# Non-local attention on one core: no scaling of probability tiles, half of the transpositions by DMA

## The reference

```python
theta = (einsum('bchw,oc->bhwo', x, w_theta) + b_theta).reshape(B, N, Ci)     # N = 1024, Ci = 64
phi   = (einsum('bchw,oc->bohw', x, w_phi) + b_phi[:, None, None]).reshape(B, Ci, N)
g     = (einsum('bchw,oc->bhwo', x, w_g) + b_g).reshape(B, N, Ci)
att   = softmax(einsum('bnc,bcm->bnm', theta, phi), axis=-1)
y     = einsum('bnm,bmc->bnc', att, g)
out   = einsum('bhwc,oc->bohw', y, w_out) + b_out
inv   = bn_gamma / sqrt(bn_var + 1e-5)
return x + out * inv + (bn_beta - bn_mean * inv)
```

## Time and profile before

| what | us |
|---|---|
| median of 3 runs (lowest, highest) | 225.02 (224.7, 225.25) |
| the profiled execution, whole | 224.65 |
| its span | 222.8 |
| PE busy in the span | 214.5 (96%) |
| DVE busy | 183.9 (83%) |
| ACT busy | 169.8 (76%) |
| POOL busy | 148.6 (67%) |
| queue that SP issues on, share of 16 DMA engines | 31.6% of the span |

### The profile page before, as it was taken

The page is one execution under the profiler, slowest core; times in us unless marked ns, Lnnn a source line. Parts: engine busy times, 40 slices in busy tenths (PEclk is TensorE's granted clock), DMA queues, the critical chain, the costliest instruction groups (busy, mean ns, idle before and its releaser), DMA issues.

```text
span 222.8 us, 4289 instructions
## 1 busy us (share of the span) xinstructions
PE 214.5 (96%) x1228; PEld 141.5 (63%) x1228; DVE 183.9 (83%) x328; ACT 169.8 (76%) x311; POOL 148.6 (67%) x143
## 2 busy tenths in 40 slices
PE   7997889999999999999999999999999999999994
PEld 6684748656665767657676666647686566656552
DVE  0789998779988699779997799797997799898761
ACT  2687977869688787869698687878878696868751
POOL 2647977786787577966787687866777843843420
PEclk9999999999999999999999999999999999999999
DMA  5107330365106531185104551085200751010102
GB/s 159 72 0 200 79 100 3 108 177 141 47 4 195 135 99 49 43 236 145 47 0 140 151 133 47 0 231 153 61 27 1 188 141 47 0 47 0 50 0 94
DMA packets 8716, 19.78 MB, mean 89 GB/s; under 512 B 1536, under 2 KB 2048, under 8 KB 8704
## 3 DMA queue, kind: packets, MB, share of 16 engines
q1 hardware_dynamic: 8416, 19.50, 31.6%
q10 hardware_dynamic: 288, 0.14, 0.2%
HBM read 4.43 MB, written 4.19 MB: 39 GB/s over the span
## 4 chain that ended last, share of the span: by engine, by line
PE 85%; DVE 6%; DMA 4%; ACT 1%; POOL 1%; issue 0%; SPq 0%; ACTq 0%; DVEq 0%
PE ps_flip L663 25%; PE ps_scores L601 25%; PE ps_y L616 12%; PE ps_y L620 8%; PE ps_misc L628 6%; PE ps_misc L687 4%; PE ps_misc L702 3%; DVE neg_max L496 2%; DMA phi_ll<-lo 2%; DMA vec<-vectors_dram 2%; DVE pt_lo L566 1%; PE ps_misc L607 1%; PE ps_misc L709 1%; DVE phi_ll L484 1%; DVE g_parts L550 1%; ACT L403 1%
## 5 line engine op out<-in xcount | busy, mean ns | idle before, releaser
L316 POOL TENSOR_SCALAR probs<-probs,inv_sum 128x1024 f32<-128x1024 f32 x64 | 72.2, 1127 | 58.3 <-DVE inv_sum L518 58.2
L566 DVE SCALAR_TENSOR_TENSOR pt_lo<-ps_flip,pt_hi 128x512 f16<-128x512 f32 x128 | 82.2, 684 | 25.3 <-ACT pt_hi L446 24.3
L446 ACT ACTIVATE pt_hi<-ps_flip 128x512 f16<-128x512 f32 x128 | 69.7, 597 | 31.6 <-PE ps_flip L663 31.5
L496 DVE TENSOR_REDUCE neg_max<-ps_scores 128x1 f32<-128x1024 f32 x64 | 77.7, 1214 | 0.6 <-PE ps_scores L601 0.5
L663 PEld LDWEIGHTS ps_flip<-ident,probs 128*128 128x128 f32 x512 | 56.9, 141 | 24.7 <-issue 10.3
L455 ACT ACTIVATE probs<-ps_scores,neg_max 128x1024 f32<-128x1024 f32 x64 | 71.8, 1122 | 0.0
L663 PE MATMUL ps_flip<-ident,probs 128*128 128x128 f32 x512 | 68.4, 277 | 3.4 <-POOL probs L316 1.6
L601 PE MATMUL ps_scores<-phi_hh,theta_hl 128*128 128x512 f32 x128 | 45.5, 436 | 0.5 <-DVE phi_ll L484 0.3
L601 PE MATMUL ps_scores<-phi_ll,theta_hl 128*128 128x512 f32 x128 | 40.1, 394 | 0.0
L616 PE MATMUL ps_y<-pt_hi,g_parts 128*128 128x512 f16 (+1 forms) x128 | 32.7, 378 | 0.0
L601 PEld LDWEIGHTS ps_scores<-phi_ll,theta_hl 128*128 128x128 f32 x128 | 24.1, 188 | 5.6
(11 more groups left out here) (77 smaller groups left out, 159.6 us busy)
## 6 DMA issues: line engine op xcount, KB each, us to landing
x_in<-x_in_dram SPq DMA_DIRECT2D x16, 256.0 KB, 3.1
out_dram<-resid SPq DMA_DIRECT2D x15, 256.0 KB, 2.0
phi_hh<-hi SPq DMA_DIRECT2D x14, 256.0 KB, 4.4
phi_ll<-lo SPq DMA_DIRECT2D x14, 256.0 KB, 4.0
theta_hl<-hi SPq DMA_DIRECT2D x7, 256.0 KB, 3.4
theta_hl<-lo SPq DMA_DIRECT2D x7, 256.0 KB, 3.1
out_dram<-resid SPq DMA_DIRECT2D x1, 192.0 KB, 2.0
w_tp<-w_tp_t_dram ACTq DMA_DIRECT2D x1, 128.0 KB, 3.4
```

Of the source, the lines that this page charges most:

```text
L316: nc.gpsimd.tensor_scalar(out=p[:, :], in0=p[:, :], scalar1=inv_sum[:, at:at + 1], scalar2=1.0, op0=ALU.mult, op1=ALU.mult).then_inc(probs ...
L446: nc.scalar.activation(pt_hi[ring][:, c * HALF_TILES:(c + 1) * HALF_TILES, slot * P:(slot + 1) * P], ps_flip[c][:, :].rearrange("p (a n) - ...
L496: nc.vector.tensor_reduce(out=neg_max[:, k % STEPS:k % STEPS + 1], in_=ps_scores[k % 2][:, :], op=ALU.max, axis=AX.X, negate=True).then_in ...
L566: nc.vector.scalar_tensor_tensor(out=pt_lo[ring][where], in0=ps_flip[c][:, :].rearrange("p (a n) -> p a n", n=P), scalar=PROB_SCALE, in1=p ...
```

## The change

Tiles are no longer multiplied by 1/sum, except the four of the last half (tiles 60 to 63), which go as before. The sum over positions is taken of unscaled probabilities, and 1/sum is applied to `y` in `scale_y`, which moves from ACT to DVE. There the 1/sum of each row n must lie along the free dimension, the same in all partitions: for each half the four columns of `inv_sum` (128x4 f32) are written by DMA to a row in DRAM, 16 bytes from each partition (`inv_to_row`), and read back into all 128 partitions (`inv_to_all`). Since a partition's four values lie together, the row is ordered (p t), and `scale_y` reads it with a stride of four.

In every half but the last, the first and third tile are flipped by DMA. For these, ln(2^15) is added to the negated maximum, so that exp gives the tile times 2^15. ACT copies it to `p_hi` in f16, POOL writes `p_lo` = tile - p_hi in f16, and SP issues a DMA transposition of each into the same `pt_hi` and `pt_lo` as before (`turn_hi`, `turn_lo`). Their 1/sum is multiplied by 2^15. The second and fourth tile are flipped by PE as before. DVE takes the reciprocals of four tiles at once. SP's loop over images becomes straight code.

```diff
+    BY_DMA = (0, 2)
+    LOG_SCALE = math.log(PROB_SCALE)
+    LAST_HALF = TILES - HALF_TILES
...
+        inv_row = [nc.dram_tensor(f"inv_row{i}", (BANK,), F32).ap() for i in range(2)]
+        p_hi = [[sbuf(f"p_hi{i}{s}", [P, N], F16) for s in BY_DMA] for i in range(2)]
+        p_lo = [[sbuf(f"p_lo{i}{s}", [P, N], F16) for s in BY_DMA] for i in range(2)]
+        inv_all = [sbuf(f"inv_all{i}", [P, BANK], F32) for i in range(2)]
...
+            def turn_hi(t):
+                if not by_dma(0, t):
+                    return
+                ring, slot = ring_of(t), t % HALF_TILES
+                wait(sp, y_ready, t // HALF_TILES - 1)
+                sp.wait_ge(p_hi_ready, move_at(0, t) + 1)
+                sp.dma_start_transpose(pt_hi[ring][:, :, slot * P:(slot + 1) * P],
+                                       p_hi[ring][BY_DMA.index(slot)][:, :]).then_inc(pt_moved[ring], 16)
...
+            def inv_to_row(h):
+                at = h * HALF_TILES % STEPS
+                sp.wait_ge(inv_sum_ready, h + 1)
+                wait(sp, inv_spread[h % 2], 16 * (h // 2))
+                sp.dma_start(inv_row[h % 2].rearrange("(p t) -> p t", p=P),
+                             inv_sum[:, at:at + HALF_TILES]).then_inc(inv_in_row, 16)
+            def inv_to_all(h):
+                sp.wait_ge(inv_in_row, 16 * (h + 1))
+                wait(sp, y_scaled, h - 1)
+                sp.dma_start(inv_all[h % 2][:, :],
+                             inv_row[h % 2].unsqueeze(0).to_broadcast([P, BANK])).then_inc(inv_spread[h % 2], 16)
             def image(it, k):
                 b, r = image_at(it, k), (k // MT) % 2
+                turn_lo(MT * b - 2)
+                inv_to_row(2 * b - 1)
                 store(it, k - 2 * MT + HALF_TILES)
+                turn_hi(MT * b)
                 if exists(b + 2, B):
                     sp.wait_ge(g_ready, b + 1)
                     sp.wait_ge(resid_ready, b + 1)
                     load_x(b + 2, r)
+                turn_lo(MT * b)
...
+                inv_to_all(2 * b - 1)
+                turn_hi(MT * b + 2)
                 store(it, k - MT)
+                turn_lo(MT * b + 2)
...
+                inv_to_row(2 * b)
+                turn_hi(MT * b + 4)
+                turn_lo(MT * b + 4)
+                inv_to_all(2 * b)
+                turn_hi(MT * b + 6)
...
                 t = tile_at(it, k - 1)
-                if exists(t, TILES):
+                if in_last_half(t) and t < TILES:
...
+                if exists(t, TILES) and by_dma(it, k - 1):
+                    hold(pt_moved[ring], moved_by(it, k - 1) - MOVED)
+                    hold(p_hi_ready, move_at(it, k - 1) + 1)
+                    nc.gpsimd.tensor_tensor(low[:, :], p[:, :], high[:, :],
+                                            ALU.subtract).then_inc(p_lo_ready, 1)
...
+                    if by_dma(it, k):
+                        high = p_hi[ring_of(k)][BY_DMA.index(k % HALF_TILES)]
+                        act.wait_ge(probs_ready, t + 1)
+                        wait(act, pt_moved[ring_of(k)], moved_by(it, k) - MOVED)
+                        nc.scalar.activation(high[:, :], probs[k % PROB_RING][:, :],
+                                             ACT.Copy).then_inc(p_hi_ready, 1)
...
+            def scale_y(h, half, r, image, spread):
+                dve.wait_ge(y_unit_ready, image + 1)
+                dve.wait_ge(inv_spread[half], spread)
+                dve.wait_ge(y_ready, h + 1)
+                nc.vector.scalar_tensor_tensor(
+                    out=y_norm[:, :].rearrange("c (t p) -> c t p", p=P),
+                    in0=ps_y[:, :].rearrange("c (t p) -> c t p", p=P), scalar=y_unit[:, r:r + 1],
+                    in1=inv_all[half][:, :].rearrange("c (p t) -> c t p", t=HALF_TILES),
+                    op0=ALU.mult, op1=ALU.mult).then_inc(y_scaled, 1)
...
-                        pe.wait_ge(pt_lo_ready, 2 * HALF_TILES * h + 2 * HALF_TILES)
+                        pe.wait_ge(pt_lo_ready, 2 * flip_at(it, k - 6 + HALF_TILES))
+                        pe.wait_ge(pt_moved[ring_of(k - 6)], moved_by(it, k - 6))
```

More of the change, by code:

```diff
@@ L24, in build_nonlocal_attention @@
 def build_nonlocal_attention(nc, x, w_tp_t, w_g_t, w_out_t, channel_vectors, out):
+    import math
     from contextlib import ExitStack
@@ L56, in build_nonlocal_attention @@
     WARM_UP = 6
+    BY_DMA = (0, 2)
+    BY_PE = tuple(slot for slot in range(HALF_TILES) if slot not in BY_DMA)
+    MOVED = 32 * len(BY_DMA)
+    LOG_SCALE = math.log(PROB_SCALE)
+    LAST_HALF = TILES - HALF_TILES
     LAST_PIECES = (slice(0, BANK - P), slice(BANK - P, BANK))
@@ L176, in build_nonlocal_attention @@
         inv_sum_ready = sem("inv_sum_ready")
+        inv_raw_ready = sem("inv_raw_ready")
+        inv_in_row = sem("inv_in_row")
+        row_max_ready = sem("row_max_ready")
+        p_hi_ready = sem("p_hi_ready")
+        p_lo_ready = sem("p_lo_ready")
+        pt_moved = [sem(f"pt_moved{i}") for i in range(2)]
+        inv_spread = [sem(f"inv_spread{i}") for i in range(2)]
         probs_scaled = sem("probs_scaled")
@@ L204, in tile_is, with in_last_half, by_dma, flip_at @@
             return isinstance(it, int) and tile_at(it, k) == t
+        def in_last_half(t):
+            return isinstance(t, int) and t >= LAST_HALF
+        def by_dma(it, k):
+            return k % HALF_TILES in BY_DMA and not in_last_half(tile_at(it, k))
+        def flip_at(it, k):
+            if in_last_half(tile_at(it, k)):
+                return LAST_HALF // HALF_TILES * len(BY_PE) + tile_at(it, k) - LAST_HALF
+            before = sum(slot < k % HALF_TILES for slot in BY_PE)
+            return it * (STEPS // HALF_TILES * len(BY_PE)) + k // HALF_TILES * len(BY_PE) + before
+        def move_at(it, k):
+            before = sum(slot < k % HALF_TILES for slot in BY_DMA)
+            return it * (STEPS // HALF_TILES * len(BY_DMA)) + k // HALF_TILES * len(BY_DMA) + before
+        def moved_by(it, k):
+            return it * (STEPS // HALF_TILES // 2 * MOVED) + (k // HALF_TILES // 2 + 1) * MOVED
+        def ring_of(k):
+            return k // HALF_TILES % 2
         def is_first(image):
@@ L271, in image @@
                     restack(phi_ll[1 - r], CI, lo, CI, 1 - r)
-            image(0, 0)
-            image(0, MT)
-            with sp.Fori(1, B // 2 - 1) as it:
+                inv_to_row(2 * b)
[3 more added lines that the diff above has]
+                turn_hi(MT * b + 6)
+            for it in range(B // 2):
                 image(it, 0)
                 image(it, MT)
-            image(B // 2 - 1, 0)
-            image(B // 2 - 1, MT)
             store(B // 2, -2 * MT + HALF_TILES)
@@ L421, in step @@
                                          bias=BIAS_TP).then_inc(proj_out, 1)
[L423 to L428, removed]
-                    scale_y(HALVES - 2, 1, ps_y[:, :], slice(0, BANK))
                 if j == 4 and exists(image + 1, B):
@@ L453, in step @@
                     act.wait_ge(max_ready, t + 1)
-                    wait(act, flipped, 2 * (t - PROB_RING) + 2)
+                    if by_dma(it, k - PROB_RING):
+                        wait(act, p_lo_ready, move_at(it, k - PROB_RING) + 1)
+                    else:
+                        wait(act, flipped, 2 * flip_at(it, k - PROB_RING) + 2)
                     nc.scalar.activation(probs[k % PROB_RING][:, :], ps_scores[k % 2][:, :], ACT.Exp,
```

79 lines of the change are left out of this document (58 added, 21 removed).

## The result

| | median us | ratio to before, 95% interval |
|---|---|---|
| before | 225.13 | |
| changed | 238.13 (237.27 to 238.92, 4 runs) | 1.0583 [1.0559, 1.0607] |

Ratios leave out runs over 1.5% above the fastest of the same kernel: six of ten of the plain moves (236.5 to 243.2 us), one of four of the first half's, and one of five of the second half's, 236.7 us, which is the run whose profile is read.

The account below looks back on a forecast made before the run. TensorE, busy 96% of the span, bounds the kernel at 25.67 us per image; a new period of 23.5 saves 2.2 us over 7.5 images, 16.5 us, so 224.65 - 16.5 = 208 us. Range 191 to 270; likeliest case 195 to 216.

Parts of the forecast that it names:

- TensorE gives up 1.06 us per tile: TensorE's flips: 30 of 64 no longer done, 31.8 us gone, leaving 21.4 us per image.
- everything is hidden: Rival: all added work and DMA hide behind TensorE, giving 193 us; chance 0.10.
- DVE, ACT and POOL: Other engines' work per image: DVE 18.6, ACT up to 20.4, POOL 19.7 to 20.9 us; none becomes the bound alone.
- A move costs 0.95 us of queue and 0.6 us of issue: Each DMA transposition on SP and its queue, priced like a plain DMA of the same 256 KB.
- sum by bytes: DMA burst: 10 plain pieces and 3 transpositions at 0.95 us, plus 2.0, make 14.4 us and a loop of 24.0.
- What is on the path: Image-to-image loop over SP, from first scores to the last restack's landing: 20.5 by issue, 20.7 by POOL, 24.0 by bytes.
- the leg to resid: Start of the loop, from an image's first scores through resid, before SP issues the x loads: 9.65 us.
- A period near the upper end, 23.5: Time per image, between 21.4 and 24.0 us, taken near the top because engines meet in order: 2.2 us saved.
- second rival: TensorE's even steps: convolution waits for scale_y behind DVE's row maximum, up to 1.0 us per half, 227 us; chance 0.08.
- The slower rival: Dear moves make SP or the queue the bound: 268 us at 3.0 us per move, 310 at 3.7; chance 0.32.
- point of decision: SP's issue per image, 7.5 + 8T, reaches 25.67 us at T = 2.3 us per move; from there SP decides.
- the signs given for this rival: Transposition issue or landing spacing over 2.3 us, SP issuing most of the span, TensorE waiting on pt_moved at every half.

Follow-up runs that it names:

- plain moves: Changed kernel with each of the 60 transpositions replaced by a plain DMA into the same places, 256-byte pieces: 1.0386 of before, some 233.4 us.
- the first half's: Changed kernel with only the first and third tile of each image's first half moved by DMA (16 tiles): 1.0752 of before, some 242.1 us.
- the second half's: Changed kernel with only the first and third tile of each image's second half moved by DMA (14 tiles): 1.0279 of before, some 231.4 us.
- everything nearly free: Changed kernel with DMA moves, ACT's copies and p_lo cut to 16 elements per partition from the second image on, scale_y reading without stride: 208.2 us.
- without moves: Changed kernel with no tile moved by DMA, reciprocal correction and move waits removed, 1/sum still applied as a row: 226.4 us, 1.0059 of before.
- fillers: Changed kernel with 12 matmuls before TensorE's restack wait: 234.8 us; with lo's restacks issued first, 9 before the move wait and 3 before the restacks: 235.8 us.
- tiny moves: Changed kernel with 52 of 60 moves, from the second image on, plain DMAs of 16 elements per partition: 217.4 us, 0.9652 of before.
- long pieces: Changed kernel with each move from the second image on a plain DMA into its own contiguous tile, 2 KB pieces: 221.5 us, 0.9858 of before.
- the kernels with fewer moves: Changed kernel moving only the first of four tiles: 1.049 of before; first and third of second halves only: 1.0279; of first halves only: 1.0752.

## Why the prediction was wrong

The steps below are those of the prediction, in its order.

1. *TensorE gives up 1.06 us per tile.* Too much. The busy time of a group counts the modelled end of the last matmul, which lies under the next instruction. From the first flip's weight load to that of the scores behind it were 0.83 and 0.87 us in the kernel before (98.92 to 99.75, 101.11 to 101.98). So 30 tiles are some 26 us, not 31.8. The kernel with everything nearly free says 25.67 - 22.69 = 2.98 us for four tiles, 0.75 each. The prediction's rival "everything is hidden" at 193 us was out of reach.
2. *DVE, ACT and POOL.* p_hi at 1.06 and p_lo at 2.14 us were as taken (1.1 and 2.3). y_norm was not: 1.14 us against 0.73, the stride's doing, 4.6 to 5.4 us in two experiments. Their sum said "none becomes the bound", which held.
3. *A move costs 0.95 us of queue and 0.6 us of issue.* **This is the step that turned the sign.** Measured: 1.69 and 1.29. The prediction had the other end right, 1,024 pieces of 256 bytes at 25 ns, 1.6 us, and chose the plain row against it. The packets say that the pieces are real: 63,360 more than without moves, 1,056 for each of 60. At about the assumed price the kernel runs in 221.5 us, at the true one in 238.1. With 13 x 0.95 replaced by 10 x 0.95 + 3 x 1.69, the prediction's own sum by bytes gives 26.2 us per image; it was 28.7 on average over the five middle images.
4. *What is on the path.* The end of the loop was right, SP's burst and the last restack, and the wait appeared where it was said to (14.6 us, seven times). Its start was not: from the second image on the burst begins with the end of the weighted sum whose buffer the first move writes (seven times), and SP waits for resid once. From an image's first scores to that move it is 8.6 us where TensorE's clock stays up, near the 9.65 taken for the leg to resid, but 10.2 to 11.3 in the four images where the clock falls behind the wait: the slow restart lies inside the loop. From the move to the last restack's landing it is 15.9 to 19.2 us, where the sum by bytes had 14.4 from the x loads on. The moves' true price is in it, and plain DMAs that take longer to issue behind them. Of this, fillers win back some 3 us for the clock.
5. *A period near the upper end, 23.5, for the order of the engines.* Even with tiny moves it was 23.9 to 24.6, and the first image, whose moves stayed real, gained nothing in any kernel that moved all its four tiles (24.3 or more against 23.16). Two places make it: scale_y behind a row maximum ahead of the convolution, the second rival's mechanism, real at 0.65 us per half rather than 1.0, and ACT's copy standing between a moved tile's exp and the flipped tile's pt_hi, which the prediction counted as busy time and not as latency (3.8 us together with POOL's subtraction). Without both it is 22.7 to 23.2, TensorE's own work.
6. *The rivals.* The slower rival named the right resource, but its point of decision (T = 2.3 us) was that of SP being busy all the time. SP had pauses of up to 6.5 us between its bursts, though its instructions took some 165 of 237 us: the loop passes through one burst that holds four moves, and T of 1.3 with a queue price of 1.7 was enough. Of the signs given for this rival, SP issuing for most of the span did appear; a median issue over 2.3 us and TensorE waiting for the moves did not.

The costs, in us, each the difference of two runs: nearly all additions nearly free 208.2; the stride 5.4, to 213.6; copies and p_lo 3.8, to 217.4; the moves' bytes in long pieces 4.1, to 221.5; the 256-byte pieces 11.9, to 233.4; the transposing 4.7, to 238.1 (the last two are one sum of 16.6, whose split rests on three runs of the plain moves, 232.8 to 234.1 us). The order in which they are added decides a little how large each is (copies 4.5 without the stride).

What stays open: which part of a move's price in this loop is SP's issue and which the queue's, since every edit changed both; how much the first move's wait for the weighted sum costs, since no run moved it behind the x loads; and whether ACT's copy explains the whole loss of the kernels with fewer moves.

Two figures that the prediction drew on, against this case. The Trainium skill, "DMA: Bandwidth & Descriptors", section Latency and other measured facts, gives a DMA transpose an effective 261 GB/s, an estimate of 1.0 us for this tile. In this kernel it was 256 KB in 1.69 us of queue, 155 GB/s, so the measurement decides against that figure here, where the destination lies in runs of 256 bytes. The Trainium skill, "VectorE: DVE Perf Modes", section The three transpose paths, gives 1309 ns for one 128x128 block by DMA. Eight blocks took 1.69 us of queue and 4.2 us to land, so blocks of one DMA do not follow one behind another at that price.

## What to carry to other kernels

Price a DMA by its pieces, not its bytes: look at the longest run that source and destination share, count the pieces and take the small-packet row of the profile; where that and the plain row differed, the piece price was the nearer one here (1.6 against 1.69 measured). When an engine is relieved and all engines would then need about the same time per image (here by the prediction within 15%), follow the loop that closes from stage to stage with each new instruction's latency and place in the order, since busy time says nothing of it: one ACT copy of 1.06 us cost 22 us more when it was moved behind the next exp, while shortening it together with POOL's subtraction won only 3.8 in the kernel with tiny moves. Before moving work to the DMA queue, draw the burst in which it will be issued, and write beside each DMA the buffer that it waits for: the first one's wait starts the whole burst.

## What the runs showed of the hardware

- Writing 128 x 4 f32 to DRAM as 512 elements of 4 bytes instead of 128 of 16: 238.1 to 322.0 us for 15 such writes; 0.3 us of one DMA engine per added packet, 7.6 us of all 16 per write of 2 KB; 0.14 us per packet in a kernel with half the moves, 231.4 to 271.0 us.
- A transposing DMA of 128x1024 f16 took 1.69 us of the queue (1.35 to 1.82 in kernels with fewer moves) and 1.23 us or more of issue; a plain one into the same places 1.45 and 0.64; into a contiguous tile 0.79 and 0.48.
- DVE's scalar_tensor_tensor of 128x512 took 1140 ns with one f32 operand read at a stride of four elements and 748 without.
- Behind an idle stretch of 2.92 us TensorE's pairs of score matmuls took 1.22 and 1.05 us; with matmuls put into the stretch, 0.61 to 0.72. Behind one of 2.30 us they were slow as well, behind one of 2.63 not.
